# The first three blocks of expert 0 listed from part of the tokens, the last set's routing moved between their products

## The chip, the cores and the metric

The kernel runs on one core of one Trainium2 chip. The metric is device time in microseconds (us) of a whole launch, the median of several runs of the same kernel on the same chip. Below, PE is TensorE, DVE is VectorE, ACT is ScalarE, POOL is GpSimd and SP is SyncE.

## What is computed

Two stages, chained and added to the input `x` (8192 tokens of 256 values):

```
ys  = cond / 16;  d = rsqrt((ys*ys) @ (w*w) + 1e-8)        # one row per batch of 64 tokens
hid = ((x * ys) @ w) * d                                     # 8192 x 256
logits = hid @ wr.T                                          # 8 experts
top 2 experts of a token; gate = softmax over the two
pos = running count of an expert's tokens, in token order; kept while pos < 2560
y = gelu(hid[tokens of e] @ w1[e] + b1[e]) @ w2[e] + b2[e]   # 256 -> 1024 -> 256
out = x + sum over its experts of gate * y
```

An expert works on its tokens in the order of the token numbers. With the reference's inputs expert 0 gets 1837 tokens, 890 of them among the first 4096 tokens and 1379 among the first 6144.

## The kernel before, in words

**Front.** The tokens go through in 16 groups (`GROUPS`) of 512, four groups to a set. For each group PE multiplies by `w` (`modulate`, L402), ACT and DVE scale the product into `hid_t` (`scale_hidden`), and PE turns it back to rows of tokens with the logits beside them (`turn_back`, L415); ACT copies those into `rows` (`copy_back`, L617). For each set DVE finds the two experts (`choose`, L793), PE counts positions (`positions`, L430), DVE makes gates (`set_gates`, L813) and slots (`find_slots`, L825), and SP stores the set's rows, gates included, in DRAM (`store_rows`, L295, into `hidden`). Then, a group at a time, DVE makes one-hot tiles of lane and column (`list_group`, L861) and PE multiplies them (`list_slots`, L450), which puts each token's number at its slot: 16 small matmuls for a group, summed in one half of PSUM bank 3 for groups 0 to 7 and in the other for 8 to 15. DVE saves the first half in `lower_list` (`save_half`, L879).

**Hand-over.** After the last group PE does the positions of set 3 and lists groups 12 to 15. DVE adds both halves into `ids` (the token number of each slot), and works out `plan`: how many blocks each expert has. Only then POOL fetches the rows of block 0 from `hidden` by an indirect DMA (`gather`, L335, three of 128 rows).

**Experts.** An expert's tokens are worked on in blocks of 384 slots; expert 0 has five, all experts together 46. PE does, for each of eight chunks f of the hidden layer, a first product (`first_product`, L493: six matmuls over 384 columns into one of three `h_bank`s, PSUM banks 4 to 6) and, three chunks behind, a second product (`second_product`, L504: nine matmuls over 256 columns into `y_bank`s 2, 3 and 7). ACT makes two gelus of each chunk (`gelu`, L666), DVE the low part (`split_chunk`, L968). In `one_block` (PE, L527) a first product waits (`bank_read`) for the gelu of the chunk three before it, whose bank it takes. The next block's rows are transposed after chunk 6's first product, and the next block's first two first products stand between the last second products of this one, so the order at a block's border is F0' S6 F1' S7 F2' F3' S0' F4' S1' F5' (F and S for first and second products, a dash for the next block). DVE adds the bias into `y` and multiplies by the gate, POOL adds the rows to the output by an indirect DMA (`adds`, L342). In blocks 0 and 1 of an expert ACT and DVE also split the next expert's weights in eight pieces, which SP has loaded into `w_raw`.

What sets the order is each engine's program, written out by hand, with semaphores between the engines. All of POOL's gathers wait for `ids_ready`; on PE the products of block 0 wait for `gathered`.

Of the kernel before, what the change touches and what calls it, by code (L numbers as in the profile page):

```python
# [16 lines left out]
P = 128  # L17
# [30 lines left out]
LEAST = 4  # L48
TILES_E = BLOCKS * SUBS
# [7 lines left out]
H_BANKS = 3  # L57
OPEN = 2
assert ROWS == 512 and T % (4 * ROWS) == 0 and BLOCKS < 16 and LEAST * SLOTS <= CAP and COLS <= 256
# [10 lines left out]
def build(nc, x, x_t, cond_t, w, wr_t, w1, b1_t, w2, b2, ident, tri, expert_low, slot_base, middle_ids, lanes,  # L70
          plan_consts, slot_consts, out):
# [4 lines left out]
    out_copy = out[0:T, :].rearrange("t d -> (t d)").rearrange("(g q r) -> g q r", g=GROUPS, q=16)  # L76
# [3 lines left out]
    with ExitStack() as ctx:  # L80
# [25 lines left out]
        plan_sb = sb("plan_consts", [P, BLOCKS + (E + 1) * E])  # L106
# [5 lines left out]
        plan = sb("plan", [P, 2 * (E + 1)], I32)  # L112
# [4 lines left out]
        ids = sb("ids", [P, COLS], I32)  # L117
# [56 lines left out]
        lane_hot = [hot_area(h_raw_sb, i, P) for i in range(HOT_RING)]  # L174
        col_hot = [hot_area(b2_sb, i, COLS) for i in range(HOT_RING)]
# [29 lines left out]
        lanes_numbered = sem("lanes_numbered")  # L205
        half_saved = sem("half_saved")
        base_step = sem("base_step")
# [33 lines left out]
        LATE = 3  # L241
# [5 lines left out]
        list_half = [list_bank[:, 0:COLS], list_bank[:, 256:256 + COLS]]  # L247
# [3 lines left out]
        HALF_AT = COUNT_AT + E  # L251
        x_bank = [bank[0], bank[1]]
        y_bank = [bank[2], bank[3], bank[7]]
        h_bank = [bank[4], bank[5], bank[6]]
# [16 lines left out]
        def _(sp):  # L271
# [18 lines left out]
            for s in range(SUBS):  # L290
                sp.dma_start(hidden[T + s * P:T + (s + 1) * P, :], empty_sb[:, :]).then_inc(pad_zero, 16)
                sp.dma_start(out[T + s * P:T + (s + 1) * P, :], empty_sb[:, 0:D]).then_inc(out_written, 16)
            load_weights(0)

            def store_rows(s):  # L295

                sp.wait_ge(rows_ready, s + 1)
                sp.dma_start(hidden[s * TS * P:(s + 1) * TS * P, :].rearrange("(j p) c -> p j c", p=P),
                             rows[s % ROW_RING][:, :, :]).then_inc(rows_stored[s % ROW_RING], 16)

            for g in range(X_RING, GROUPS):
                sp.wait_ge(m_done, KC * (g - X_RING + 1))
                load_x(g)
                if g == X_RING + 2:
                    for tile, src in ((plan_sb[:, :], plan_consts), (b1_sb[:, :], b1_t),
                                      (slot_sb[:, :, :], slot_consts.rearrange("p (v t) -> p v t", v=3))):
                        sp.dma_start(tile, src).then_inc(late_in, 16)
# [4 lines left out]
            for g in range(GROUPS - X_RING, GROUPS):  # L312
                copy_x(g)
            store_rows(SETS - 1)
            sp.wait_ge(t_done, 1)
            sp.dma_start(b2_sb[:, :], b2.rearrange("e d -> (e d)").partition_broadcast(P)).then_inc(b2_in, 16)
# [11 lines left out]
        def _(pool):  # L328
# [6 lines left out]
            def gather():  # L335
                for s in range(SUBS):
                    pool.indirect_dma_start(  # L337
                        xg[:, s, :], None, hidden,
# [18 lines left out]
            def next_block(k, tile):  # L357
# [16 lines left out]
            gather()  # L374
            next_block(1, SUBS)
            pool.wait_ge(out_written, out_filled)
            pool.wait_ge(plan_ready, 1)
            _, end = plan_of(pool, 0)
            with pool.Fori(0, end - LAG) as b:
                next_block(b + LAG, (b + LAG) * SUBS)  # L380
                adds(b)
            with pool.Fori(1, E) as e:
# [3 lines left out]
                with pool.Fori(start, start + both % 16 + LEAST) as b:  # L386
                    next_block(b + LAG, e * TILES_E + (b - start) * SUBS)
# [6 lines left out]
        def _(pe):  # L394
# [35 lines left out]
            def positions(s):  # L430
# [4 lines left out]
                if s == SETS // 2:  # L435
                    pe.matmul(pos_bank[:, HALF_AT:HALF_AT + E], ones_sb[:, :], before[:, :], start=True, stop=True)
# [13 lines left out]
            def list_slots(g):  # L450

                if g == GROUPS // 2:
                    pe.wait_ge(half_saved, 1)
                pe.wait_ge(lanes_numbered, g + 1)
                pe.wait_ge(cols_ready, g + 1)
                for c in range(TOP_K):
                    for j in range(TILES):
                        mm = pe.matmul(list_half[g * 2 // GROUPS], lane_hot[g % HOT_RING][:, c, :, j],
                                       col_hot[g % HOT_RING][:, c, :, j],
                                       start=(g * 2 % GROUPS == 0 and c == 0 and j == 0),  # L460
                                       stop=((g + 1) * 2 % GROUPS == 0 and c == TOP_K - 1 and j == TILES - 1))
# [42 lines left out]
            def second_product(u, f):  # L504

                cols = slice(WCOLS + f * D, WCOLS + (f + 1) * D)
                for s in range(SUBS):
                    hi = h_hi[f % RING][:, s * P:(s + 1) * P]
                    lo = h_lo[f % RING][:, s * P:(s + 1) * P]
                    y = y_bank[s][:, 0:D]  # L510
                    pe.matmul(y, hi, w_hi[u][:, cols], start=(f == 0), stop=False)  # L511
                    pe.matmul(y, hi, w_lo[u][:, cols], start=False, stop=False)  # L512
                    mm = pe.matmul(y, lo, w_hi[u][:, cols], start=False, stop=(f == FC - 1))  # L513
# [13 lines left out]
            def one_block(u, u_next, b, weights=None):  # L527

                first_product(u, 2)
                for f in range(3, FC):  # L530
                    bank_read(b, f - 3)
# [7 lines left out]
                    second_product(u, f - 3)  # L539
                chunk_split(b, FC - 3)  # L540
# [15 lines left out]
            pe.wait_ge(gathered, 16 * SUBS)  # L556
            transpose_block()
            pe.wait_ge(w_lo_done, PIECES)
# [4 lines left out]
            pe.wait_ge(plan_ready, 1)  # L563
# [8 lines left out]

            _, end = plan_of(pe, 0)
            expert(0, 0, 0, end)
# [9 lines left out]
        def _(act):  # L584
# [56 lines left out]

            act.wait_ge(set_dve, 10)
            scale_hidden(0)
            for g in range(GROUPS):
# [4 lines left out]
                if g % JOINED == 0 and g > 0:  # L649
                    odds(g // JOINED - 1)  # L650
                copy_back(g)
# [3 lines left out]
            def split_rows(b):  # L655

                act.wait_ge(t_done, b + 1)
                for k in range(KC):
                    act.copy(xt_hi[:, k * SLOTS:(k + 1) * SLOTS], x_bank[k][:, 0:SLOTS]).then_inc(xt_hi_done, 1)  # L659

# [3 lines left out]
            split_rows(0)  # L664
# [28 lines left out]
            bias(0, 0)  # L693
            act.wait_ge(plan_ready, 1)
            _, end = plan_of(act, 0)
            expert(0, 0, 0, end)
# [13 lines left out]
        def _(dve):  # L710
# [150 lines left out]
            def list_group(g):  # L861

                dve.wait_ge(lanes_found, g // JOINED + 1)
                if g >= HOT_RING:
                    dve.wait_ge(listed, g - HOT_RING + 1)
                hot = lane_hot[g % HOT_RING]
                one_hot(hot, P, lane_of, g).then_inc(lanes_ready, 1)
                one_hot(col_hot[g % HOT_RING], COLS, col_of, g).then_inc(cols_ready, 1)
# [10 lines left out]
            def save_half():  # L879
# [4 lines left out]
                                  list_half[0].rearrange("p (e t) -> p e t", e=E), over_experts(1),  # L884
                                  ALU.add).then_inc(half_saved, 1)

            for g in range(GROUPS):
# [5 lines left out]
                if g == GROUPS // 2 + 5:  # L893
                    save_half()
                if g % JOINED == 0 and g > 0:
                    choose(g // JOINED - 1)
                if g % JOINED == 1 and g > JOINED:
                    find_slots(g // JOINED - 1)
                    set_gates(g // JOINED - 1)
                if g % JOINED == 2 and g > JOINED:  # L900
# [5 lines left out]
            choose(SETS - 1)  # L906
            set_gates(SETS - 1)
            find_slots(SETS - 1)
            for g in range(GROUPS - JOINED, GROUPS):
                list_group(g)  # L910
# [159 lines left out]
```

## Time and profile before

| | |
|---|---|
| median of 3 runs | 974.43 us (974.03 to 974.87) |
| profiled execution, its own time | 976.05 us |
| its span | 974.2 us |
| PE busy | 932.7 us, 96% |
| ACT busy | 539.6 us, 55% |
| DVE busy | 470.1 us, 48% |
| POOL busy | 390.7 us, 40% |
| mean granted TensorE clock | 0.98 of full |
| DMA | 82.04 MB, 84 GB/s |

The page's second part cuts the span in 40 slices of 24.4 us; PE's row is 6 in the first, 9 in nearly all others and 4 at the end, with 9s again for the granted clock. The lower digits of a short stretch vanish in such slices, so the time around the hand-over, 118 to 150 us, is read in windows and instruction by instruction.

### The profile page before, as it was taken

To read this page: it belongs to the slowest core of one execution; us is meant where nothing else is said; L and a number is where in the kernel's file an instruction comes from. 1 tells how busy PE (TensorE), PEld (TensorE's weight loads), DVE (VectorE), ACT (ScalarE), POOL (GpSimd) and SP (SyncE) were. 2 spreads that over 40 slices of the span, in tenths; PEclk is the share of its full clock that TensorE was granted. 3 is DMA by queue.
4 is the path that set the end of the run, shared out by engine and by line. 5 is a ranking of instruction groups with operands and counts; after the bars stand their busy time and mean duration, and the time that the engine had idled before them with its cause. 6 is when DMAs were issued, how large, how long until landed. Compare 5 with 4: busy or idle time off the path is not lost.

```text
span 974.2 us, 19276 instructions
## 1 busy us (share of the span) xinstructions
PE 932.7 (96%) x6402; PEld 891.0 (91%) x6403; DVE 470.1 (48%) x1068; ACT 539.6 (55%) x1231; POOL 390.7 (40%) x419
## 2 busy tenths in 40 slices
PE   6999939999999999999999999999999999999994
PEld 3666629999999999999999999999999999999994
DVE  3488765435543354344533454445334544343341
ACT  6877606555655565556555565565555655555551
POOL 0000012545445355454553544545535445455333
PEclk9999959999999999999999999999999999999998
DMA  9566543622443225222532234225322322223222
GB/s 324 178 220 218 176 131 138 135 37 52 69 107 48 39 50 132 41 50 44 134 45 38 49 53 121 49 44 135 45 38 49 49 38 49 44 50 45 37 33 33
DMA packets 53402, 82.04 MB, mean 84 GB/s; under 512 B 6592, under 2 KB 42432, under 8 KB 52992
## 3 DMA queue, kind: packets, MB, share of 16 engines
q0 software_dynamic: 26496, 36.76, 23.3%
q1 hardware_dynamic: 25328, 44.42, 13.6%
q10 hardware_dynamic: 1552, 0.53, 0.2%
q8 instruction: 13, 0.21, 0.1%
q14 instruction: 13, 0.11, 0.0%
HBM read 54.16 MB, written 35.93 MB: 92 GB/s over the span
## 4 chain that ended last, share of the span: by engine, by line
PE 84%; issue 14%; POOL 1%; DMA 0%; DVE 0%; POOLq 0%; DVEq 0%
PE bank L511 14%; PE bank L512 14%; PE bank L513 13%; PE bank L499 13%; PE bank L500 13%; PE bank L501 13%; PE bank L489 3%; POOL out_rows L350 0%; DMA sb_xg<-hidden,sb_gather_ids 0%; POOL sb_xg L337 0%; DVE sb_y L997 0%; DVE sb_y L1003 0%; POOL sb_add_ids L347 0%; POOL sb_gather_ids L332 0%; POOL sb_ids_ring L333 0%
## 5 line engine op out<-in xcount | busy, mean ns | idle before, releaser
L670 ACT ACTIVATE sb_h_raw<-bank,sb_b_now 128x384 f32<-128x384 f32 x368 | 215.0, 584 | 280.6 <-PE bank L501 280.5
L971 DVE TENSOR_TENSOR sb_h_lo<-sb_h_raw,sb_h_hi 128x384 fp32r<-128x384 f32 x368 | 205.3, 558 | 319.6 <-ACT sb_h_hi L670 319.4
L511 PE MATMUL bank<-sb_w_hi,sb_h_hi 128*128 128x256 f32 x1104 | 314.8, 285 | 0.0
L512 PE MATMUL bank<-sb_w_lo,sb_h_hi 128*128 128x256 f32 x1104 | 311.3, 282 | 0.0
L513 PE MATMUL bank<-sb_w_hi,sb_h_lo 128*128 128x256 f32 x1104 | 309.7, 281 | 0.0
L499 PE MATMUL bank<-sb_xt_hi,sb_w_hi 128*128 128x384 f32 x736 | 250.0, 340 | 1.7 <-issue 1.7
L500 PE MATMUL bank<-sb_xt_lo,sb_w_hi 128*128 128x384 f32 x736 | 249.9, 339 | 0.0
L501 PE MATMUL bank<-sb_xt_hi,sb_w_lo 128*128 128x384 f32 x736 | 249.6, 339 | 0.0
L350 POOL DMA_INDIRECT out_rows<-sb_y,sb_add_ids x138 | 221.5, 1605 | 67.8 <-POOL sb_add_ids L347 37.9
L670 ACT ACTIVATE sb_h_hi<-bank,sb_b_now 128x384 fp32r<-128x384 f32 x368 | 212.7, 578 | 0.0
L513 PEld LDWEIGHTS bank<-sb_w_hi,sb_h_lo 128*128 128x128 f32 x1104 | 208.3, 189 | 0.0
L511 PEld LDWEIGHTS bank<-sb_w_hi,sb_h_hi 128*128 128x128 f32 x1104 | 207.8, 188 | 0.0
L512 PEld LDWEIGHTS bank<-sb_w_lo,sb_h_hi 128*128 128x128 f32 x1104 | 207.5, 188 | 0.0
L332 POOL COPY sb_gather_ids<-sb_ids 128x3 int32 (+1 forms) x46 | 11.2, 244 | 389.3 <-DVE sb_gates L940 255.0
L337 POOL DMA_INDIRECT sb_xg<-hidden,sb_gather_ids x138 | 136.8, 991 | 67.5 <-POOL sb_ids_ring L333 39.3
L499 PEld LDWEIGHTS bank<-sb_xt_hi,sb_w_hi 128*128 128x128 f32 x736 | 138.8, 189 | 2.0 <-issue 2.0
L500 PEld LDWEIGHTS bank<-sb_xt_lo,sb_w_hi 128*128 128x128 f32 x736 | 138.9, 189 | 0.0
L501 PEld LDWEIGHTS bank<-sb_xt_hi,sb_w_lo 128*128 128x128 f32 x736 | 138.9, 189 | 0.0
L659 ACT CAST sb_xt_hi<-bank 128x384 fp32r<-128x384 f32 x92 | 39.8, 486 | 101.2 <-PE bank L501 79.5
L931 DVE TENSOR_TENSOR sb_xt_lo<-bank,sb_xt_hi 128x384 fp32r<-128x384 f32 x92 | 47.0, 553 | 83.2 <-ACT sb_xt_hi L659 83.2
L997 DVE TENSOR_TENSOR sb_y<-bank,sb_b 128x256 f32<-128x256 f32 x138 | 50.1, 418 | 43.6 <-PE bank L513 43.6
L411 PE MATMUL bank<-sb_x,sb_w 128*128 128x512 f32 x128 | 59.5, 608 | 0.5 <-ACT sb_hid_t L639 0.4
(112 smaller groups left out, 583.0 us busy)
## 6 DMA issues: line engine op xcount, KB each, us to landing
sb_w_raw<-in_w SPq DMA_DIRECT2D x16, 1024.0 KB, 7.9
hidden<-sb_rows SPq DMA_DIRECT2D x4, 2112.0 KB, 9.2
sb_x<-in_x_t SPq DMA_DIRECT2D x16, 512.0 KB, 4.4
out_rows<-in_x SPq DMA_DIRECT2D x16, 512.0 KB, 5.6
sb_xg<-hidden,sb_gather_ids POOLq DMA_INDIRECT x138
out_rows<-sb_y,sb_add_ids POOLq DMA_INDIRECT x138, 3.8
sb_b<-in_b SPq DMA_DIRECT2D x1, 1024.0 KB, 4.9
hidden<-sb_empty SPq DMA_DIRECT2D x3, 132.0 KB, 8.2
```

The lines of the kernel that those rows point to most:

```text
L337: pool.indirect_dma_start(xg[:, s, :], None, hidden, bass.IndirectOffsetOnAxis(gather_ids[:, s:s + 1], axis=0),).then_inc(gathered, 16)
L350: pool.indirect_dma_start(out, bass.IndirectOffsetOnAxis(add_ids[:, s:s + 1], axis=0), y[s][:, :], None, compute_op=ALU.add,).then_inc(add ...
L411: mm = pe.matmul(m_bank[c % M_RING][:, :], w_sb[:, k, o * P:(o + 1) * P], x_in[g % X_RING][:, k, :], start=(k == 0), stop=(k == KC - 1))
L499: pe.matmul(h, w_hi[u][:, cols], xt_hi[:, rows], start=(k == 0), stop=False)
L500: pe.matmul(h, w_hi[u][:, cols], xt_lo[:, rows], start=False, stop=False)
L501: mm = pe.matmul(h, w_lo[u][:, cols], xt_hi[:, rows], start=False, stop=(k == KC - 1))
L511: pe.matmul(y, hi, w_hi[u][:, cols], start=(f == 0), stop=False)
L512: pe.matmul(y, hi, w_lo[u][:, cols], start=False, stop=False)
L513: mm = pe.matmul(y, lo, w_hi[u][:, cols], start=False, stop=(f == FC - 1))
L670: ins = act.activation(h, h_bank[f % H_BANKS][:, 0:SLOTS], ACT.Gelu_apprx_tanh, bias=b1_now[u][:, f:f + 1])
L971: dve.tensor_tensor(h_lo[f % RING][:, :], h_raw[f % RING], h_hi[f % RING][:, :].bitcast(F32), ALU.subtract).then_inc(h_ready, 1)
L997: dve.tensor_tensor(y[s][:, :], y_bank[s][:, 0:D], b2_sb[:, bass.ds(e * D, D)], ALU.add).then_inc(y_read, 1)
```

## The change

It starts the first three blocks of expert 0 before all tokens are routed, and moves the last set's routing between the products of these blocks.

1. The list of slots has three parts (groups 0 to 7, 8 to 11, 12 to 15). After the first, at g = 13, DVE makes the ids of blocks 0 and 1 (`list_two_blocks`), and POOL gathers from the stored sets 0 and 1 alone; the third block's ids come after group 11 is listed (`list_third_block`). A block with fewer known tokens than slots would be filled with spare rows altogether (`short`) and one more block added at the end (`missing`).
2. PE's order after group 15's `modulate` is: wait for the gather of block 0, its transposes, `turn_back(15)`, lists 10 and 11, F0, F1, `positions(3)`, and three unrolled blocks, with lists 12 and 13 in block 0 and 14 and 15 in block 1 (before: `turn_back(15)`, lists 10 and 11, `positions(3)`, lists 12 to 15, gather, transposes, F0, F1). PE waits for `plan_ready` only before block 3, ACT and DVE before block 2, POOL before gather 3.
3. DVE does set 3's gates, slots and one-hots between the chunks of blocks 0 and 1, and then `base_of_slots` and `plan_blocks` (the same work as before with three small instructions more). `save_half` stands behind `find_slots` and `set_gates` at g = 13.
4. PSUM: two `h_bank`s (4 and 5) for three; `y_bank`s 0 and 1 share bank 2, the third is in bank 6; banks 3 and 7 stay with the lists and positions.
5. The next expert's weights are split in blocks 2 and 3 of expert 0 (before: 0 and 1); SP loads them after the second transposes, and `b2` before storing set 3. The spare rows of `hidden` and of the output stand in front.

```diff
-H_BANKS = 3
+H_BANKS = 2
-        y_bank = [bank[2], bank[3], bank[7]]
-        h_bank = [bank[4], bank[5], bank[6]]
+        y_bank = [bank[2][:, 0:D], bank[2][:, 256:256 + D], bank[6][:, 0:D]]
+        h_bank = [bank[4], bank[5]]
...  (SP)
+            sp.wait_ge(listed, LAST_SET)
+            sp.dma_start(b2_sb[:, :], ...).then_inc(b2_in, 16)
             store_rows(SETS - 1)
-            sp.wait_ge(t_done, 1)
-            sp.dma_start(b2_sb[:, :], ...).then_inc(b2_in, 16)
+            sp.wait_ge(t_done, 2)
...  (POOL)
-            pool.wait_ge(ids_ready, 1)
+            pool.wait_ge(early_ready, 1)
             list_block(0, 0)
             pool.wait_ge(pad_zero, 16 * SUBS)
-            for i in range(ROW_RING):
-                pool.wait_ge(rows_stored[i], 16 * (SETS // ROW_RING))
+            pool.wait_ge(rows_stored[0], 16)
+            pool.wait_ge(rows_stored[1], 16)
             pool.wait_ge(gather_listed, 1)
-            gather()
-            next_block(1, SUBS)
+            gather(2)
+            next_block(1, SUBS, 2)
             pool.wait_ge(out_written, out_filled)
+            pool.wait_ge(early_ready, 2)
+            pool.wait_ge(rows_stored[0], 32)
+            next_block(2, 2 * SUBS, 3)
+            adds(0)
+            pool.wait_ge(ids_ready, 1)
             pool.wait_ge(plan_ready, 1)
+            pool.wait_ge(rows_stored[1], 32)
...
-            with pool.Fori(0, end - LAG) as b:
-                next_block(b + LAG, (b + LAG) * SUBS)
+            with pool.Fori(1, end - LAG) as b:
+                next_block(b + LAG, (b - 1 + filled) * SUBS + EARLY_TILES)
                 adds(b)
...  (PE, one_block)
+                bank_read(b, 0)
                 first_product(u, 2)
                 for f in range(3, FC):
-                    bank_read(b, f - 3)
+                    bank_read(b, f - 2)
                     first_product(u, f)
...
                     second_product(u, f - 3)
+                    if isinstance(b, int) and b < 2 and f % 2 == 1 and f >= 5:
+                        list_slots(LAST_SET + 2 * b + (f - 5) // 2)
...  (PE, after group 15)
-            turn_back(GROUPS - 1)
-            list_slots(GROUPS - 6)
-            list_slots(GROUPS - 5)
-            positions(SETS - 1)
-            for g in range(GROUPS - JOINED, GROUPS):
-                list_slots(g)
...
             pe.wait_ge(gathered, 16 * SUBS)
             transpose_block()
+            turn_back(GROUPS - 1)
+            list_slots(LAST_SET - 2)
+            list_slots(LAST_SET - 1)
...
             for f in range(OPEN):
                 first_product(0, f)
-            pe.wait_ge(plan_ready, 1)
+            positions(SETS - 1)
...
+            for b in range(EARLY):
+                one_block(0, 0, b)
+            pe.wait_ge(plan_ready, 1)
             _, end = plan_of(pe, 0)
-            expert(0, 0, 0, end)
+            expert(0, 0, EARLY, end)
...  (DVE)
+            def list_two_blocks():
+                dve.wait_ge(half_counted, 1)
+                dve.wait_ge(half_saved, 1)
+                dve.tensor_tensor(early_ids[:, few], lower_list[:, few], slot_sb[:, 2, few], ALU.add)
+                early_mark(dve.tensor_tensor(short[:, few], early_sb[:, few], known(HALF_AT, FEW), ALU.is_gt), 1)
+                early_mark(dve.scalar_tensor_tensor(spare[:, few], short[:, few], -NO_SLOT, ...), 2)
+                whole(dve.tensor_tensor, ids[:, few], early_ids[:, few], spare[:, few], ALU.min).then_inc(early_ready, 1)
...
             split_rows(0)
             take_gates(0, first=True)
-            for f in range(2):
-                split_chunk(0, f)
+            choose(SETS - 1)
+            set_gates(SETS - 1)
+            split_chunk(0, 0)
+            find_slots(SETS - 1)
+            split_chunk(0, 1)
+            list_third_block()
...  (DVE, one_block)
                     split_chunk(b, f)
+                    if isinstance(b, int) and b < 2 and f in (2, 4):
+                        list_group(LAST_SET + 2 * b + f // 2 - 1)
+                    if isinstance(b, int) and b == 1 and f == 5:
+                        base_of_slots()
...
+                if isinstance(b, int) and b == 1:
+                    plan_blocks()
...
-                    dve.wait_ge(y_done, b * SUBS + (s + 1))
+                    dve.wait_ge(y_done, b * SUBS + max(s + 1, 2))
```

On ACT the copies of block 0's transposed rows (`split_rows(0)`) stand ahead of `copy_back(15)`; the load of the gelu table and its first use stand behind the exponentials of set 3, as before.

## Rows read from the trace of the kernel before

**Rows 1.** Windows: busy us of PE, PEld, DVE, ACT, POOL, clock, DMA share, GB/s.

```profile
120.00:130.00 10.00, 3.74 (x50) 2.89 (x50) 9.41 (x24) 1.37 (x2) 0.00 (x0) 0.60 0.65 216
```

**Rows 2.** PE in order of time: start, duration, line, tiles, idle before and releaser.

```profile
114.49 0.41 PE L424 MATMUL bank<-sb_back,sb_hid_t 128*128 128x136 f32 x2
...
116.36 2.61 PE L458 MATMUL bank<-sb_b,sb_h_raw 128*128 128x168 f16 x16
120.89 0.56 PE L439 MATMUL bank<-sb_mask,sb_ones 128*128 128x8 bf16 x16 [1.92 <-DVE sb_mask L811]
...
121.89 0.22 PE L447 MATMUL bank<-sb_before,sb_ones 128*128 128x128 bf16 x1
...
141.54 1.54 PE L489 MATMUL bank<-sb_back,sb_xg 128*128 128x128 f32 x6 [7.33 <-DMA sb_xg<-hidden,sb_gather_ids]
144.75 0.66 PE L499 MATMUL bank<-sb_xt_hi,sb_w_hi 128*128 128x384 f32 x1 [1.67 <-issue]
...
162.41 0.34 PE L499 MATMUL bank<-sb_xt_hi,sb_w_hi 128*128 128x384 f32 x1
...
180.10 0.34 PE L499 MATMUL bank<-sb_xt_hi,sb_w_hi 128*128 128x384 f32 x1
```

**Rows 3.** DVE in order of time, 104 to 137 us.

```profile
104.39 0.29 DVE L821 TENSOR_TENSOR sb_rows<-sb_picked 128x128 f32<-128x128 f32 x1
...
116.97 0.29 DVE L797 TENSOR_REDUCE sb_top<-sb_rows 128x16 f32<-128x128 f32 x1 [1.36 <-ACT sb_rows L624]
...
124.55 0.19 DVE L850 SCALAR_TENSOR_TENSOR sb_lane_of<-sb_col_of,sb_slot_of 128x32 f16<-128x32 f16 x1
...
126.15 0.68 DVE L871 TENSOR_TENSOR sb_h_raw<-sb_h_raw,sb_middle_ids 128x1024 f16<-128x1024 f16 x1
...
134.38 0.33 DVE L769 TENSOR_TENSOR sb_ids<-bank,sb_upper 128x168 int32<-128x168 f32 x1
...
136.25 0.17 DVE L769 TENSOR_SCALAR sb_plan<-sb_plan_f 128x9 int32<-128x9 f32 x1
```

**Rows 4.** ACT in order of time, 119 to 122 us.

```profile
119.65 0.22 ACT L629 ACTIVATE sb_ratio<-sb_gap 128x16 f32<-128x16 f32 x1 [2.71 <-DVE sb_gap L806]
...
121.18 0.20 ACT L663 ACTIVATE sb_warm<-sb_empty 128x1 f32<-128x1 f32 x1
```

**Rows 5.** POOL in order of time: the last of three gathers, blocks 0 and 1.

```profile
138.77 0.95 POOL L337 DMA_INDIRECT sb_xg<-hidden,sb_gather_ids  x1 [0.30 <-issue]
...
148.54 0.98 POOL L337 DMA_INDIRECT sb_xg<-hidden,sb_gather_ids  x1 [0.30 <-issue]
```

**Rows 6.** DMA queue in 141.0 to 141.5 us: packets, MB, share of 16 engines.

```profile
q0 software_dynamic: 12, 0.00, 3.3%
```

**Rows 7.** DMA queues in 146 to 150 us.

```profile
q1 hardware_dynamic: 407, 1.63, 100.0%
```

**Rows 8.** DMA queues in 153.5 to 154.0 us.

```profile
q0 software_dynamic: 29, 0.05, 34.1%
```

**Rows 9.** DMA queues in 106 to 118 us.

```profile
q1 hardware_dynamic: 2093, 4.17, 103.7%
```

**Rows 10.** PE at a block's border, 415 to 418 us.

```profile
415.43 0.34 PE L499 MATMUL bank<-sb_xt_hi,sb_w_hi 128*128 128x384 f32 x1
...
416.49 0.28 PE L511 MATMUL bank<-sb_w_hi,sb_h_hi 128*128 128x256 f32 x1
...
417.57 0.34 PE L499 MATMUL bank<-sb_xt_hi,sb_w_hi 128*128 128x384 f32 x1
```

**Rows 11.** ACT beside it: the second gelus of chunks 1 and 2.

```profile
413.98 0.58 ACT L670 ACTIVATE sb_h_hi<-bank,sb_b_now 128x384 fp32r<-128x384 f32 x1
...
416.11 0.57 ACT L670 ACTIVATE sb_h_hi<-bank,sb_b_now 128x384 fp32r<-128x384 f32 x1
```

**Rows 12.** DVE beside it: the three additions into y.

```profile
413.92 1.09 DVE L997 TENSOR_TENSOR sb_y<-bank,sb_b 128x256 f32<-128x256 f32 x3 [0.90 <-PE bank L513]
```

**Rows 13.** ACT at the start of expert 1.

```profile
232.99 0.21 ACT L684 COPY sb_b_now<-sb_b 128x8 f32 x1
```

More of the change, by code:

```diff
@@ L116, in build @@
         lower_list = sb("lower_list", [P, COLS])
-        ids = sb("ids", [P, COLS], I32)
+        ids = sb("ids", [P, EARLY_TILES + COLS], I32)
+        short = sb("short", [P, EARLY_TILES])
+        spare = sb("spare", [P, EARLY_TILES])
+        early_ids = sb("early_ids", [P, EARLY_TILES])
+        missing = sb("missing", [P, 1])
         ys_t = sb("ys_t", [P, KC, B])
@@ L246, in build @@
         list_bank = bank[3]
-        list_half = [list_bank[:, 0:COLS], list_bank[:, 256:256 + COLS]]
+        list_part = [list_bank[:, i * COLS:(i + 1) * COLS] for i in range(3)]
         back_bank = [bank[4], bank[5], bank[6]]
@@ L457, in list_slots @@
                     for j in range(TILES):
[L458 to L461, printed above, removed]
+                        mm = pe.matmul(list_part[part], lane_hot(g)[:, c, :, j],
+                                       col_hot(g)[:, c, :, j],
+                                       start=(g in (0, 2 * JOINED, LAST_SET) and c == 0 and j == 0),
+                                       stop=(g + 1 in (2 * JOINED, LAST_SET, GROUPS) and c == TOP_K - 1 and j == TILES - 1))
                 mm.then_inc(listed, 1)
@@ L509, in second_product @@
                     lo = h_lo[f % RING][:, s * P:(s + 1) * P]
[L510 to L513, printed above, removed]
+                    y = y_bank[s]
+                    pe.matmul(y, hi, w_hi[u][:, cols], start=(f == 0 and s != 1), stop=False, skip_group_check=True)
+                    pe.matmul(y, hi, w_lo[u][:, cols], start=False, stop=False, skip_group_check=True)
+                    mm = pe.matmul(y, lo, w_hi[u][:, cols], start=False, stop=(f == FC - 1), skip_group_check=True)
                     if f == FC - 1:
@@ L640, in scale_hidden, with split_rows @@
                 ins.then_inc(hid_lower, 1)
+            def split_rows(b):
+                act.wait_ge(t_done, b + 1)
+                for k in range(KC):
+                    act.copy(xt_hi[:, k * SLOTS:(k + 1) * SLOTS], x_bank[k][:, 0:SLOTS]).then_inc(xt_hi_done, 1)
             act.wait_ge(set_dve, 10)
@@ L653, in _ @@
                     split_piece(0, g - 2, 32)
[L655 to L659, printed above, removed]
             odds(SETS - 1)
@@ L693, in _ @@
             bias(0, 0)
+            for b in range(EARLY - 1):
+                one_block(0, 0, b, None)
             act.wait_ge(plan_ready, 1)
             _, end = plan_of(act, 0)
-            expert(0, 0, 0, end)
+            expert(0, 0, EARLY - 1, end)
             with act.Fori(0, E // 2 - 1) as pair:
@@ L883, in save_half, with known @@
                 dve.tensor_tensor(lower_list[:, :].rearrange("p (e t) -> p e t", e=E),
-                                  list_half[0].rearrange("p (e t) -> p e t", e=E), over_experts(1),
+                                  list_part[0].rearrange("p (e t) -> p e t", e=E), over_experts(1),
                                   ALU.add).then_inc(half_saved, 1)
+            def known(at, n):
+                return pos_bank[:, at:at + 1].to_broadcast([P, n])
+            FEW = 2 * SUBS
+            few, more = slice(0, FEW), slice(FEW, EARLY_TILES)
@@ L899, in _ @@
                     set_gates(g // JOINED - 1)
+                if g == GROUPS // 2 + 5:
+                    save_half()
+                    list_two_blocks()
                 if g % JOINED == 2 and g > JOINED:
@@ L905, in _ @@
                     list_group(g - 4)
[L906 to L910, printed above, removed]
-            totals = pos_bank[:, COUNT_AT:COUNT_AT + E]
-            dve.tensor_tensor(valid[:, :, :], totals.unsqueeze(2).to_broadcast(EC), over_experts(0), ALU.is_gt)
-            dve.tensor_tensor(upper[:, :, :], pos_bank[:, HALF_AT:HALF_AT + E].unsqueeze(2).to_broadcast(EC),
-                              over_experts(0), ALU.is_le).then_inc(base_step, 1)
@@ L1010, in expert @@
                     one_block(u, e, b, None)
+            for b in range(EARLY - 1):
+                one_block(0, 0, b, None)
             _, end = plan_of(dve, 0)
-            expert(0, 0, 0, end)
+            expert(0, 0, EARLY - 1, end)
             with dve.Fori(0, E // 2 - 1) as pair:
```

194 lines of the change are left out of this document (129 added, 65 removed).

## The prediction, made before the changed kernel ran

> **What bounds the kernel now.** I read the page's slices first: PE is at 9 tenths from the second slice to the last but one, so what doesn't show as idle PE time saves nothing. Then the windows around the hand-over: in 120 to 130 us PE is busy 3.7 of 10 us and its clock is 0.60 of full, falling to the half level, 1.2 GHz [rows 1]. Then PE in order of time: lists 10 and 11 end at 118.97, positions run 120.89 to 122.11, the transposes wait until 141.54 for the gather, and the first product F0 starts at 144.75 [rows 2]. The reader sees one hole of 25 us with little in it but routing. DVE shows what fills it: `choose` from 116.97, the one-hots to 126.83 for the first group and on for three more, `ids` at 134.38, `plan` done at 136.42 [rows 3]; then POOL's three gathers, the last issued at 138.77 [rows 5]. Behind the hole PE never stops: F0 of blocks 1 and 2 start at 162.41 and 180.10, a period of 17.69 us [rows 2], and expert 1 begins at 232.99 [rows 13], which is (232.99 - 144.75)/17.69 = 5.0 blocks. So the time is the front, the hole, 46 block periods and a tail.
>
> **The change, step by step.** All times are on the clock of the trace of before.
>
> *Early ids.* At g = 13 `set_gates` ends at 104.68 [rows 3]. Behind it now stand `save_half` (0.3) and three small instructions handed on by semaphore (10 such, from `ids` to `plan`, take 134.38 to 136.42, so 0.2 each [rows 3]): the early ids start at 105.4. From `ids` to the third gather's issue it took 138.77 - 134.38 = 4.4 [rows 3, 5], so now 109.8.
>
> *The gather lands among other DMAs.* Undisturbed, the last packets of the third gather moved 2.2 to 2.7 us after its issue and PE started 2.8 after it [rows 2, 5, 6]: 112.6. But the store of set 2 and four copies keep the engines full from 106 to 118 us (103.7% by q1 alone) [rows 9]. The nearest row: block 1's gathers met the loads of weights; q0 moved nothing at all in 146 to 150 us, q1 had 100.0% [rows 7], and the third gather, issued at 148.54, still had packets in 153.5 to 154 [rows 5, 8], 5.5 us after issue for 2.8. I take 109.8 + 5.5 = 115.3. Bounds: 112.6, and 118.4 if it is served only as q1 runs dry. PE comes free for the transposes at 114.5, where `turn_back(15)` started [rows 2], so the wait costs 0.8 (0 to 3.9), and everything behind it on PE, `turn_back(15)` and with it `choose` for set 3, is as late.
>
> The Trainium skill (DMA: Bandwidth & Descriptors, Queues, rings and completion order) says that an engine takes turns between its queues packet by packet. By that rule the gather would get a turn beside each packet of q1 and land at about 113, at no wait, and the total would be 0.8 us lower; the trace disagrees in 146 to 150 us, where q0 had no turn. The sum goes by the rows.
>
> *PE up to F0.* Six transposes 0.6 at full clock (half of an undisturbed 1.54 and less, for the overlap), to 115.9; `turn_back(15)` 1.9 (114.49 to 116.36) to 117.8; lists 10 and 11 2.5 (the row says 2.61 to its end) [rows 2]: F0 at 120.3 instead of 144.75, **24.45 us earlier**. ACT's and DVE's part for block 0 (two copies, two subtractions) lies beside `turn_back(15)` and the lists.
>
> *The clock.* Before, F0 to F0' of block 0 took 162.41 - 144.75 = 17.66. That stretch lacks the two second products of a block before, 2 x 1.07 [rows 10], so it should be 15.54; the other **2.1 us** were lost to the half clock, at which the first product lasted 0.66 for 0.34 [rows 2]. Now PE has no idle stretch over 1 us, so the clock should stay and this comes back.
>
> *What goes in between PE's products.* Positions, 120.89 to 122.11: **1.2**. Four lists: two took 2.5 at full clock [rows 2], so **5.0**.
>
> *Waits in block 0.* `choose` starts at 118.5 (2.5 after `turn_back(15)` starts, plus 0.1, as in the old trace [rows 2, 3]), the mask is done 3.9 later (positions waited for it until 120.89 [rows 2]) at 122.4, just as F0 and F1 (2.1) end; positions to 123.6. ACT's warm-up of the gelu ended at 121.38, 4.4 after `choose` started [rows 3, 4]: now 122.9, the bias copy 0.2 more, gelu 0 done at 124.2, gelu 1 at 125.3 (two activations of 0.58 each, overlapping by 0.1 [rows 11]). F2 needs gelu 0 now that there are two banks: **0.6 wait**. F3 follows at 125.3. Queued on DVE: split 0 to 124.8; `find_slots` 2.4 (from the end of positions, 122.11, to 124.74 it took 2.6 with the hand-over [rows 2, 3]) to 127.2; split 1 to 127.7; the third block's ids, nine small instructions, 1.9, to 129.6; split 2 to 130.1; the one-hots of group 12, 126.83 - 124.74 = 2.1 [rows 3], to 132.2. PE meanwhile: F3, S0, F4, S1, F5, S2 to 131.6, then it waits for group 12: **0.5**. List 12, F6, T, S3, F7, S4, list 13, S5, and F0' of block 1 at 140.6. Group 13's one-hots (done by 135.2, wanted at 138.3) and those of block 1, which begin with no backlog and have 2.1 us of PE work to each, come before PE wants them. F0 of block 2: 140.6 + 17.69 + 2.5 = 160.8 for 180.10.
>
> *The plan.* `plan_ready` needs list 15 (about 159) and then 2.3 us of DVE: 161.8. ACT's next gelu is wanted at 161.9 and its result by 165: covered, 3 us to spare. POOL's gather 3 goes out behind it, 161.8 + 1 for registers + 4.4, landed by 170; PE wants it in block 2 after F6 at about 173.5. Covered by 3.
>
> *Two h banks, 46 blocks.* The tight places are F3' and F4', which now need gelus 1' and 2'. These end at 414.56 and 416.68 [rows 11]; F3' and F4' start at 415.43 and 417.57 [rows 10]: 0.87 and 0.89 to spare. Cost nothing (up to 0.4 a block if every gelu slipped by over 1 us, which no row shows).
>
> *Shared y bank.* DVE's first addition waits for one third more of S7, 0.36; the three (1.09 [rows 12]) then end at about 415.4, before PE wants them at 416.49 [rows 10]. In the last block nothing hides it: **0.36 late**. The weights load later (t_done 2, about 135) yet 20 us before their first use; `b2` and the store of set 3 have as much room.
>
> *Sum.* 24.45 + 2.1 - 1.2 - 5.0 - 0.6 - 0.5 = 19.25 (and 180.10 - 160.8 = 19.3); less 0.36: 18.9. The profiled execution took 976.05, span 974.2 plus 1.85 around it: 957.1 by its own time. It lies 1.6 above the runs' median of 974.43, so the runs should say **955.5**.
>
> The Trainium skill (SBUF — State Buffer, its part on which operations grab the shared pair) says that a DVE instruction with two SBUF inputs and a GpSimd instruction that reads SBUF shut each other out. By that rule the early gathers, which now fall on DVE's one-hots of groups 8 and 9, could be issued 1 to 2 us later. The third gather of block 1 overlapped a DVE subtraction of that kind and took 0.98 for 0.95 [rows 5], so the trace doesn't show it.
>
> **Rivals.**
>
> *A late gather.* It lands at 118.4, when q1 is dry. For it: q0's four empty us [rows 7], and copies in large packets at the end (2093 packets for 4.17 MB [rows 9]). Price: 3.1 more, and PE idle for 3.9 us lets the clock fall as it did after 118.97 [rows 1, 2], another 2: 960.6.
>
> *DVE becomes the bound.* From 122.4 to 132.2 its queue has no gap; each us that the nine handed-on instructions or the splits take more delays list 12 and all behind it. If they take half as long again, with list 13 late too: 2 to 3 us, 958.
>
> *Two banks stall every block (the other side).* If the hand-over PE to ACT to PE at F3' and F4' took 1.2 longer than it does now, each would wait 0.3, 0.6 a block, 46 x 0.6 = 27.6: 983.1, slower. It decides above 18.9/46 = 0.41 a block. Against it: the margins of 0.87 and 0.89, the same in every block read.
>
> *Short blocks.* If expert 0 had under 768 tokens among the first 4096, or under 1152 among 6144, a block of spare rows would be added: 17.69 back, 973.2, no change. The inputs give 890 and 1379, so only a fault in the planning would do it.
>
> *Better.* The gather in time and no DVE wait: 954.2.
>
> **How the numbers follow.** Forecast as summed, 954.3 to 957.5: 0.60. Better: 0.06. Late gather or a fallen clock, 957.5 to 961: 0.17. DVE: 0.10. Two banks, or something as large in each block: 0.05. Short block: 0.02. The range, 953.8 to 960, leaves out the last two and a part of the second rival. A difference under 0.2%, 1.9 us, can't be told from none; faster by more 0.93, same 0.02, slower 0.05.
>
> **What would show it.** F0 near 120, and block 2's F0 near 161; PE's wait on the gather under 1 us; the clock at 1.00 from 110 us on; one PE wait on ACT before F2 and one on DVE before list 12, each under 1 us; L499's idle time zero in later blocks and the period still 17.69; 46 blocks (368 gelus of each kind). Wrong if the transposes start after 117, if the clock shows 0.5 after 115, or if PE waits for L670 in a block past the third.

## The result: 12.5 us faster, 6.7 us above the forecast time

| | before | changed |
|---|---|---|
| median | 974.65 us (4 runs, 974.03 to 975.76) | 962.17 us (4 runs, 961.31 to 963.66) |
| profiled execution, span | 976.05, 974.2 | 961.9, 959.7 |
| ratio | | 0.9872, 95% interval 0.986 to 0.9885 |

The time lies outside the forecast range of 953.8 to 960.0; the forecast was 955.5.

PE in the changed kernel, in order of time. The first product of block 0 starts at 125.27 and not near 120 (144.75 before [rows 2]). The transposes start at 117.96, after a wait of 4.88 us, and last 1.54 us, as they did at the half clock [rows 2]:

```profile
110.47 2.61 PE L499 MATMUL bank<-sb_b,sb_h_raw 128*128 128x168 f16 x16
112.90 0.19 PE L526 MATMUL bank<-sb_before,sb_ones 128*128 128x8 bf16 x1
117.96 1.54 PE L532 MATMUL bank<-sb_back,sb_xg 128*128 128x128 f32 x6 [4.88 <-DMA sb_xg<-hidden,sb_gather_ids]
119.30 0.66 PE L464 MATMUL bank<-sb_back,sb_hid_t 128*128 128x136 f32 x2
...
125.27 0.46 PE L542 MATMUL bank<-sb_xt_hi,sb_w_hi 128*128 128x384 f32 x1
...
129.20 0.44 PE L542 MATMUL bank<-sb_xt_hi,sb_w_hi 128*128 128x384 f32 x1 [0.50 <-ACT sb_h_hi L726]
...
145.16 0.34 PE L542 MATMUL bank<-sb_xt_hi,sb_w_hi 128*128 128x384 f32 x1
...
165.30 0.34 PE L542 MATMUL bank<-sb_xt_hi,sb_w_hi 128*128 128x384 f32 x1
```

Windows of the same trace (columns as in [rows 1]). The clock falls in the wait and is at the half level through nearly all of `turn_back(15)`:

```profile
112.00:114.00 2.00, 1.08 (x9) 0.68 (x6) 2.00 (x3) 0.00 (x0) 0.00 (x0) 1.00 1.33 561
114.00:116.00 2.00, 0.00 (x0) 0.00 (x0) 0.02 (x1) 0.00 (x0) 0.00 (x0) 1.00 0.83 329
116.00:118.00 2.00, 0.04 (x1) 0.04 (x1) 0.00 (x0) 0.00 (x0) 0.00 (x0) 0.54 0.41 99
118.00:120.00 2.00, 2.00 (x10) 2.00 (x11) 0.00 (x0) 0.46 (x2) 0.00 (x0) 0.50 0.00 0
120.00:122.00 2.00, 2.00 (x10) 2.00 (x10) 1.11 (x3) 1.16 (x4) 0.31 (x2) 0.50 0.00 0
122.00:124.00 2.00, 2.00 (x13) 1.68 (x13) 0.40 (x2) 0.76 (x2) 1.26 (x2) 0.76 0.00 0
```

GpSimd's early gather, three pieces (before, the third piece of each block took 0.95 and 0.98 [rows 5]):

```profile
105.51 1.73 POOL L370 DMA_INDIRECT sb_xg<-hidden,sb_gather_ids  x1 [0.94 <-POOL sb_ids_ring L366]
107.54 1.48 POOL L370 DMA_INDIRECT sb_xg<-hidden,sb_gather_ids  x1 [0.30 <-issue]
109.33 0.95 POOL L370 DMA_INDIRECT sb_xg<-hidden,sb_gather_ids  x1 [0.31 <-issue]
```

And the DMA queues in three stretches, 108 to 112, 112 to 116 and 116 to 118 us (packets, MB, share of 16 engines). q1 carries SP's DMAs, here the store and the copies, as in [rows 9]; q0 carries GpSimd's, here the gather. No packet of q0 shows in the first stretch, though two pieces were issued by 109.0; 66 of the 144 move in the second, beside the copies, and 78 only in the last:

```profile
q1 hardware_dynamic: 716, 1.25, 104.8%
...
q1 hardware_dynamic: 96, 1.57, 94.3%
q0 software_dynamic: 66, 0.21, 13.7%
...
q0 software_dynamic: 78, 0.20, 40.0%
q1 hardware_dynamic: 16, 0.00, 0.5%
```

Behind block 0 PE's times are as forecast: 20.14 us from F0' to F0 of block 2 (forecast 20.19, before 17.69 without the two lists [rows 2]), no idle PE in any later block, expert 1 at 218.17 for 232.99 [rows 13], 368 gelus of each kind. One margin was thinner than forecast: ACT had to wait for the plan until 167.41 before block 2's first gelu, whose product was done at 166.5. PE didn't wait for it.

### The profile page after: what moved, and what is told of

Same layout as the page of the kernel before. It is cut to its first block, busy times and chain, and to the rows that moved or that the text cites. A ratio compares the mean times of both kernels' runs of the same rounds, so it can differ in the third digit from the quotient of the medians.

```text
span 959.7 us, 19188 instructions
## 1 busy us (share of the span) xinstructions
PE 930.3 (97%) x6403; PEld 889.7 (93%) x6404; DVE 469.6 (49%) x1083; ACT 538.0 (56%) x1231; POOL 394.0 (41%) x419
## 4 chain that ended last, share of the span: by engine, by line
PE 86%; issue 12%; DMA 1%; POOL 1%; ACT 0%; DVE 0%; POOLq 0%; DVEq 0%
PE bank L555 14%; PE bank L556 14%; PE bank L557 14%; PE bank L542 13%; PE bank L543 13%; PE bank L544 13%; PE bank L532 3%; DMA sb_xg<-hidden,sb_gather_ids 1%; PE bank L499 1%; POOL out_rows L383 0%; POOL sb_xg L370 0%; PE bank L466 0%; PE bank L464 0%; ACT sb_h_raw L726 0%; ACT sb_h_hi L726 0%
## 5 line engine op out<-in xcount | busy, mean ns | idle before, releaser
L383 POOL DMA_INDIRECT out_rows<-sb_y,sb_add_ids x138 | 224.9, 1630 | 67.8 <-POOL sb_add_ids L380 36.2
L365 POOL COPY sb_gather_ids<-sb_ids 128x3 int32 (+1 forms) x46 | 8.7, 189 | 360.9 <-DVE sb_gates L1068 232.2
```

What stands on the lines that cost most here:

```text
L383: pool.indirect_dma_start(out, bass.IndirectOffsetOnAxis(add_ids[:, s:s + 1], axis=0), y[s][:, :], None, compute_op=ALU.add,).then_inc(add ...
```

## Experiments

I held three theories of the late gather. Q: its packets are served after what q1 was given before. P: DVE's one-hots keep GpSimd from writing its descriptors, the list of what the DMA engines are to move. S: it is q1's packets of 1 KB, which the store has and the copies don't, that starve q0. And, for the rest of the missing 6 us, the two banks might cost something.

**The copies ahead of the store of set 2.**

```diff
-            store_rows(SETS - 2)
             for g in range(GROUPS - X_RING, GROUPS):
                 copy_x(g)
+            store_rows(SETS - 2)
```

> The changed kernel with the last four copies of x into the output issued ahead of the store of set 2 (at about 83 us, when the DMA queues fall idle) instead of behind it. Theory Q (the early gather is served only after what q1 was given before it): only the store, done at about 110 us, stands before the gather; it lands at 112.5 to 113.5, PE waits under 1 us for it, the clock stays at full, F0 at 118 to 119 instead of 125.3, and the time is 955 to 956.5 against 962.2. Theory P (DVE's one-hots keep GpSimd from writing the gather's descriptors, two of three issues took 1.73 and 1.48 us for 0.98): nothing about DVE or GpSimd is changed, so the gather still lands near 118 and the time stays at 962. Theory S (packets of 1 KB in q1, which the store has, are what starves q0): the gather lands after 112 but not before; 956 to 957.

Measured: **954.42 us** (953.82 to 954.66), ratio 0.9787 (0.9772 to 0.9802). PE no longer waits for the gather; the wait for gelu 0 is there as before, 0.49 us:

```profile
113.09 0.85 PE L532 MATMUL bank<-sb_back,sb_xg 128*128 128x128 f32 x6
...
118.06 0.46 PE L542 MATMUL bank<-sb_xt_hi,sb_w_hi 128*128 128x384 f32 x1
...
121.99 0.44 PE L542 MATMUL bank<-sb_xt_hi,sb_w_hi 128*128 128x384 f32 x1 [0.49 <-ACT sb_h_hi L726]
```

Its DMA queues in 107 to 110 and 110 to 112 us: nothing of q0 up to 110 us, while the store runs, then 142 of its 144 packets in 2 us, as the store ends:

```profile
q1 hardware_dynamic: 930, 0.98, 104.6%
q14 instruction: 1, 0.01, 0.6%
...
q0 software_dynamic: 142, 0.40, 61.6%
q1 hardware_dynamic: 154, 0.15, 22.9%
```

GpSimd's pieces still took 1.74, 1.48 and 0.94, so P is out as the cause of the lateness, and what q1 has been given is the cause, as Q says. Expert 1 starts at 210.98 for 218.17: 7.19 us, of which 4.87 is the transposes' start (117.96 to 113.09) and the rest the half clock (transposes to F0 7.31 against 4.97).

**The store of set 2 behind the transposes**, the copies in the store's old place (all given out by 106.93).

```diff
-            store_rows(SETS - 2)
+            sp.wait_ge(rows_ready, SETS - 1)
             for g in range(GROUPS - X_RING, GROUPS):
                 copy_x(g)
+            sp.wait_ge(t_done, 1)
+            store_rows(SETS - 2)
```

> The changed kernel with the store of set 2 issued only after the transposes of block 0; the four copies stay where they were in time. Theory Q: only the copies (2.1 MB read and written, about 6 us) stand before the gather; it lands at 112 to 114, time 955 to 957. Theory P: unchanged, 962. Theory S (the store's small packets starve q0, not the copies): q0 moves packets at once, from 107.5 us on, and lands at 112; 955. If copies of 32 KB rows alone hold the gather back as long as both did, it lands after 115 and the time is over 958.

Measured: 955.90 us (954.90 to 956.09). PE waited 0.29 us for the gather. q0 moved nothing until 111 us, its first piece issued by 108.8, so the copies, in packets of 16 KB, hold it back too, and theory S falls. Either half of the traffic may stay; both together don't fit.

**Both moves.**

> Both: copies ahead, store of set 2 behind the transposes, so that no other DMA runs beside the early gather. Theory Q: the gather lands 2.8 us after its last issue as in the kernel before, at 112.1, before PE comes free for it at 112.9; no wait, F0 at 118.0, clock at full throughout, time 962.2 - 7.2 = 955.0. Theory P: the descriptors are as late as before, so the last issue still ends at 110.3; if they were the cause PE would still wait to 118 and the time stay at 962. This is also the candidate for the best version.

Measured: 954.40 us (953.83 to 955.82); transposes at 112.91, no wait. Forecast to 0.6 us, and no better than the copies alone, since PE comes free for them only then.

**The banks alone, in the kernel before.**

```diff
-H_BANKS = 3
+H_BANKS = 2
...
-        h_bank = [bank[4], bank[5], bank[6]]
+        y_bank = [bank[2][:, 0:D], bank[2][:, 256:256 + D], bank[6][:, 0:D]]
+        h_bank = [bank[4], bank[5]]
...  (PE's and DVE's waits for these banks, as in the changed kernel)
```

> The kernel before with only the banks of the changed one: two h banks (first products wait for the gelu two chunks back), y banks 0 and 1 in one bank, DVE's first addition waiting for two. My prediction: block period 17.69 as before, only the tail 0.36 later: 974.4 + 0.4 = 974.8, ratio 1.0004. Rival (the banks cost something in each block): over 0.1 us in each of 46 blocks, 979 or more, and PE idle before the first products in the trace.

Measured: 978.16 us (11 runs, 976.45 to 978.64), ratio 1.0027 (1.0018 to 1.0036): 2.6 us slower, neither forecast nor rival. (The medians are 3.3 apart, which is too much: the runs of both kernels fall in two groups, told of at the end, and more of these lay in the slower one.) The trace has one place where PE waits that the kernel before doesn't have, in block 0, and none later. PE and ACT there:

```profile
156.29 0.44 PE L499 MATMUL bank<-sb_xt_hi,sb_w_hi 128*128 128x384 f32 x1 [1.66 <-ACT sb_h_hi L671]
```

```profile
154.67 0.62 ACT L616 CAST sb_w_hi<-sb_w_raw 128x512 fp32r<-128x512 f32 x1 [3.56 <-DMA sb_w_raw<-in_w]
155.19 0.57 ACT L671 ACTIVATE sb_h_raw<-bank,sb_b_now 128x384 f32<-128x384 f32 x1
155.66 0.57 ACT L671 ACTIVATE sb_h_hi<-bank,sb_b_now 128x384 fp32r<-128x384 f32 x1
```

ACT stands at a piece of the next expert's weights, which arrive late there, with gelu 3 queued behind. In the kernel before ACT stands there too, until 154.66, and PE doesn't wait: a third bank covered that delay, two don't. PE's product at 156.29 started at 154.30 before, 2.0 us earlier, and expert 1 starts at 235.10 for 232.99 [rows 13], 2.1 us. With 0.3 at the tail (DVE's last additions start at 962.07 for 959.66) that is the 2.5 between the spans (976.7 and 974.2), but for 0.1. The changed kernel splits these weights two blocks later, from 171.75 on, where ACT doesn't wait for them, and doesn't pay it.

**The copies behind the first piece of the gather.** Two forms; in the first the signal is GpSimd's own increment:

```diff
+                    if tell:
+                        pool.sem_inc(piece_issued, 1)
...
+            sp.wait_ge(piece_issued, 1)
             for g in range(GROUPS - X_RING, GROUPS):
                 copy_x(g)
```

> The changed kernel in which SP gives the four copies out only after GpSimd has issued the first of the three pieces of the early gather (a semaphore of its own), so that the first piece (issued by 107.3 us) stands before the copies in time and the second and third (109.0 and 110.3) behind one to three of them. If the DMA engines serve the queues in the order in which the work was given to them, q0 moves its first 48 packets as soon as the store is through, at 109.5 to 111, before the copies, and the third piece is as late as ever, 116 to 118. If q0 is served only when q1 is dry, no q0 packet moves before about 116. If the queues took turns packet by packet, all three pieces would be through by 113. PE's wait ends with the third piece.

Measured: 964.07 us, one run. Not conclusive: the increment came before the issue began, SP gave the copies out from 107.2 us, the piece was issued from 107.4 to 109.2, and q0 moved first at 113. In the second form a memset of GpSimd behind the DMA gives the signal.

> As the run in which the copies wait for the first piece of the early gather, but the signal comes from a memset of GpSimd that stands behind that piece's DMA instruction, so that it can't come before the piece is issued (in that run it came as the issue began). SP gives the four copies out from then on. Served in the order of giving: q0's first 48 packets move when the store's packets end, before any copy packet, and the second and third pieces between or behind the copies. Served only when q1 leaves room: q0's first packets come after the first copies' packets, as in the run before. PE waits for the third piece in either case: 962 to 965.

Measured: 962.36 us, one run; the first piece issued at 107.5, the copies given out from 107.6, as late as in the changed kernel or later. Its queues in 110 to 112 us:

```profile
q1 hardware_dynamic: 189, 0.69, 107.8%
q0 software_dynamic: 48, 0.14, 22.1%
```

The 48 packets of the first piece moved right at the end of the store and among the first copy's packets, 2 us earlier than in the changed kernel, where two or three copies had been given out before it was issued; the third piece still came last (PE's wait ended at 118.41). That is what serving in the order of giving makes. It is one run, and a stretch of the kernel before speaks against it as a general rule (below): for this place supported, not settled.

**DVE made to wait for GpSimd's increments**, on the kernel with both moves. The increments stand behind the three pieces, as in the first form above; they were meant to hold DVE until the pieces are issued.

```diff
                 dve.wait_ge(lanes_found, g // JOINED + 1)
+                if g == 2 * JOINED:
+                    dve.wait_ge(piece_issued, SUBS)
```

> Both DMA moves of the run before (copies ahead, store of set 2 behind the transposes), and DVE holds its one-hots of group 8 until GpSimd has issued the three pieces of the early gather. If DVE's one-hots (two inputs from SBUF) are what stretched the first two issues to 1.74 and 1.48 us, all three now take 0.95 to 1.0 us, the last issue ends 1.2 us earlier; if not, they take what they took. The time is longer, since DVE starts its lists about 3.5 us later: PE waits for lists 8 and 9, 956 to 959.

Measured: 955.99 us, one run. The pieces:

```profile
107.15 1.17 POOL L372 DMA_INDIRECT sb_xg<-hidden,sb_gather_ids  x1 [0.93 <-POOL sb_ids_ring L368]
108.62 1.04 POOL L372 DMA_INDIRECT sb_xg<-hidden,sb_gather_ids  x1 [0.30 <-issue]
109.97 1.04 POOL L372 DMA_INDIRECT sb_xg<-hidden,sb_gather_ids  x1 [0.30 <-issue]
```

They took 3.25 us in sum for 4.16. But the hold ended before the second piece began, since all three increments had come by then. DVE's first one-hot:

```profile
108.12 0.69 DVE L919 TENSOR_TENSOR sb_h_raw<-sb_lanes,sb_lane_of 128x1024 f16<-128x1024 f16 x1 [1.65 <-POOLq L377]
```

So the first piece alone had no one-hot beside it, but for its last 0.2 us, and took 1.17 us for 1.74. The second had them beside it as before and took 1.04 for 1.48; the third took 1.04 for 0.94. That the one-hots stretched the first piece by 0.6 us fits; that they stretch every piece that they stand beside is refuted, and why the second was shorter stays open. None of it cost PE anything here. My forecast that PE would wait for lists 8 and 9 was wrong, as the hold lasted about 2 us and not 3.5: it started them at 112.12, as the other kernels with the clock's early fall (below) did.

**PE's wait last**, DMAs as in the changed kernel.

```diff
-            pe.wait_ge(gathered, 16 * SUBS)
-            transpose_block()
             turn_back(GROUPS - 1)
             list_slots(LAST_SET - 2)
             list_slots(LAST_SET - 1)
+            pe.wait_ge(gathered, 16 * SUBS)
+            transpose_block()
...  (ACT: copy_back(15) ahead of split_rows(0); DVE: choose(3) ahead of split_rows(0))
```

> The changed kernel with its DMAs as they are (the gather late, at 118), but PE waits for it only after turn_back(15) and lists 10 and 11, with ACT's copy_back(15) and DVE's choose(3) likewise ahead of the split of the transposed rows. If the loss came from what is queued on PE behind the wait, and from the clock that falls while it waits: PE works 113 to 117.4, waits under 1 us, the clock stays at full, F0 at 120.7 instead of 125.3, and the wait for the first gelu is gone: 957.2 against 962.2. If only the landing of the gather mattered, the time stays at 962.

Measured: 959.34 us (958.48 to 961.43), ratio 0.9833 (0.9818 to 0.9848): 2.8 us better than the changed kernel, not 5. The trace is one with the clock's early fall (below), so its times are 1.5 us late against those of the changed kernel.

```profile
120.77 0.87 PE L532 MATMUL bank<-sb_back,sb_xg 128*128 128x128 f32 x6 [1.77 <-DMA sb_xg<-hidden,sb_gather_ids]
123.32 0.66 PE L542 MATMUL bank<-sb_xt_hi,sb_w_hi 128*128 128x384 f32 x1 [1.67 <-issue]
```

The work that had stood behind the wait was now done before it ended, but nothing lies between the transposes and F0 any more: the split of the transposed rows (2.55 us from one to the other) is bare, and F0 runs at the half clock after all.

**The idle stretch at 41 us.** On the kernel with the copies ahead, `turn_back(4)` before `positions(0)`; then also ACT's first exponential behind `copy_back(4)`.

```diff
+                if g == JOINED + 1:
+                    turn_back(g - 1)
                 if g % JOINED == 1 and g > JOINED:
                     positions(g // JOINED - 1)
-                turn_back(g - 1)
+                if g != JOINED + 1:
+                    turn_back(g - 1)
```

> The kernel with the copies ahead (954.4 us), and turn_back(4) ahead of positions(0), in the place where PE was idle from 40.8 to 42.9 us in all kernels and where the profile of the kernel before shows the clock at 0.50 from 43.7 to 47 us (the others don't). Theory: 1.9 us of idle filled and, since PE is busy without a break from there to the hand-over, 1.9 us gained, 952.5; and the two groups into which the runs of the kernel before fall (974.0 to 974.9 and 975.6 to 976.3) go, as the clock has no reason to fall there. Rival: find_slots(0) on DVE comes 0.9 us later and passes it on, gain under 0.5 us.

Measured: 953.61 us (5 runs, 953.42 to 953.99), 0.8 gained of 1.9. PE's wait for the most part only moved (1.49 us for 2.05), behind ACT's table load (1.28 us):

```profile
43.83 0.50 PE L464 MATMUL bank<-sb_back,sb_hid_t 128*128 128x136 f32 x2 [1.49 <-ACT sb_rows L682]
```

> The kernel with copies ahead and turn_back(4) ahead of positions(0) (953.6 us), and ACT's first exponential, whose table load of 1.28 us stood before copy_back(4), behind those copies. In the trace of that kernel PE's fourth tile of turn_back(4) waited 1.5 us for them. Theory: the wait goes and PE has no idle stretch there: 1.4 us less, 952.2. Rival: set_gates(0) and the store of set 0 come later and pass it on: no gain, 953.6. In both no run stands 1.6 us above the others, as in the kernel before, if it is the clock's fall after that idle stretch that made them.

Measured: **953.18 us** (5 runs, 953.06 to 953.36), ratio 0.9784 (0.977 to 0.9797): 0.4 more, not 1.4, since a wait of 0.66 for ACT came up in the next group's `turn_back`. It is the fastest run here, 9.0 us below the changed kernel.

## Why the prediction was wrong

The step that failed is "The gather lands among other DMAs": "I take 109.8 + 5.5 = 115.3 ... so the wait costs 0.8". And with it "Now PE has no idle stretch over 1 us, so the clock should stay". Two of the prediction's own signs of being wrong came: the transposes started after 117, and the clock stood at the half level after 115.

The front of the trace of before is 1.6 us slower than that of the changed kernel (why is below), so the forecast's 115.3 is 113.7 on the new clock. Then, step by step:

- **Landing.** 117.96 for 113.7: 4.3 late. Of that 1.1 is the issue (109.33 for 108.2), mostly since the first two pieces took 1.73 and 1.48 us and not 1.17 and 0.98, as those of block 0 did before; the other 3.1 is that 8.6 us passed from issue to the end of the wait where I took 5.5. The row I took it from [rows 7, 8] met other traffic: the last of 3 MB of weights, which were through 5.5 us after the issue. What decided here was how much had been given to q1 before the last piece, the store and all four copies: without either of the two the wait was gone or 0.29 us. My upper bound, "served only as q1 runs dry", was nearer, but not the right value either: 118.4 is 116.8 on the new clock, and PE started 1.2 later. Nor was q0 shut out until q1 ran dry, as 66 of its packets moved beside the copies.
- **Clock.** Transposes to F0 took 7.3 for 5.0: 2.3 more, the half clock. I had priced it at 2 in the rival. With the gather on time the same stretch took 4.97.
- **From F0 on.** F0 to block 2's F0 took 40.03 for 40.5: 0.5 less. The wait for gelu 0 was there (0.50 for 0.6), the one of 0.5 for group 12's one-hots wasn't. The 1.2, 5.0 and 2.1 of positions, lists and the old clock loss held.
- **Tail.** Block 2's F0 moved by 14.8 us and the span by 14.5: 0.3 for the shared y bank, forecast 0.36.

4.3 + 2.3 - 0.5 = 6.1 of the 6.7 between forecast and median. Of the other 0.6, 0.3 is that the profiled execution took 2.2 us beyond its span and not 1.85, and 0.3 that the median lies above it, which is within the spread of the runs. The outcome is the mechanism of the rival of a late gather, to which I gave 0.17 and 960.6; the time lies above its bounds too (957.5 to 961), as it was priced with the issue on time. With the gather on time (copies ahead) the same sum is right to 1.1 us: 954.4 for 955.5, and for 954.2 of the case "Better".

Two banks cost nothing in the changed kernel but the forecast wait for gelu 0 and the tail, but my reason was too wide: I looked at the margin in settled blocks, and block 0 of the kernel before would have shown that there the third bank hides a late DMA.

The two rules. The first is that the DMA engines take turns between the queues packet by packet (the Trainium skill, DMA: Bandwidth & Descriptors, Queues, rings and completion order). The changed kernel and the one with the copies ahead show no such turn while the store's 1 KB packets run, though two pieces were issued; had I built on it there, I would have missed by more. But the trace of the kernel before has a stretch that I didn't read, right behind [rows 7]. From 150 to 153.5 us q0 moved 115 packets beside 911 of q1, and SP had given out the last of these by 144.45, before the gather's first piece was issued (from 146.01):

```profile
143.98 0.47 SPq L281 DMA_DIRECT2D sb_w_raw<-in_w  x1
...
q1 hardware_dynamic: 911, 0.93, 80.8%
q0 software_dynamic: 115, 0.35, 28.0%
```

So q0 doesn't always wait for all that q1 was given before it. Neither rule, turns from the first packet on or the order of giving, fits every trace here. What the runs show is that the traffic of q1 made this gather late and that moving half of it away cured that; how the packets of the two queues are put in order stays open.

The second is that a DVE instruction with two SBUF inputs and a GpSimd instruction that reads SBUF shut each other out (the Trainium skill, SBUF — State Buffer, Who interferes with whom). I set it aside by one overlap, of 0.16 us at the start of the issue (the subtraction ran from 148.14 to 148.70), too short to show anything. The early pieces beside the one-hots took 1.73 and 1.48 us, and the third was issued 1.1 us late, about what I had said that rule would make. But the third took 0.95 beside a one-hot, and a second piece took 1.04 in the run where DVE waited for the increments: the rule alone doesn't tell which pieces are stretched, and that stays open.

## What to carry over

Before an early start is credited, look at what the DMA queues have been given by the moment of its gather: a small transfer on another queue may wait for most of it, and then the cheapest cure is to move the traffic that nobody waits for into an idle stretch. A wait in an in-order queue costs more than itself: here 4.9 us, in which the ready work behind it stood still, and 2.3 us more for the clock that fell meanwhile. Before a wait is added as a hold, read in the trace when it ended: an increment behind a DMA instruction may come before that instruction's issue. A spare bank that does nothing in settled blocks may be covering a late DMA in the first one.

## What the runs showed that I had not expected

The runs of the kernel before fall in two groups, 974.0 to 975.1 and 975.6 to 976.3. The profiled executions show a likely cause: PE idles for 2.05 us at 41 us, before `positions(0)`, and in some executions the clock falls behind it. The window of 43 to 48 us in the kernel before, and the same in the changed one:

```profile
43.00:48.00 5.00, 5.00 (x36) 4.52 (x36) 1.04 (x2) 2.25 (x7) 0.00 (x0) 0.66 0.43 171
```

```profile
43.00:48.00 5.00, 5.00 (x39) 3.59 (x40) 2.48 (x7) 3.90 (x14) 0.00 (x0) 1.00 0.46 177
```

Ten executions of kernels with that stretch were profiled; in the six with 0.66 to 0.67 PE starts lists 8 and 9 at 112.0 to 112.4, in the four with 1.00 at 110.4 to 110.7. (My expectation of `turn_back(4)` first says that the kernel before alone shows the fall; it is one of six.) So the profiled execution of before was 1.6 us above its median for a cause in its own trace, and I could have read it there. In the two kernels that shorten the stretch the ten runs lie within 0.6 us of each other in each; that the second group is gone for good is likely and not shown by so few.
